# Weighed heads sent through DRAM, and a group's row shifts turned by one transpose and joined through DRAM

## The reference, cut to what matters

```
n = layernorm(x)
q, k, v = n @ Wq.T + bq, n @ Wk.T + bk, n @ Wv.T + bv        # 32 heads of 16
q, k = rope(rope(q, absolute), temporal), rope(rope(k, absolute), temporal)
w = softmax(causal(q @ k.T / 4))
x = x + layernorm((w @ v) @ Wo.T + bo)
x = x + layernorm(ffn(layernorm(x)))                          # gate, up, silu, down
```

## Time and profile before

| | |
|---|---|
| median of 3 runs | 2745.22 us |
| the profiled execution | 2745.2 us, its span 2743.5 us |
| PE / DVE / ACT / POOL busy | 92% / 77% / 52% / 36% of the span |
| attention phase | from the start to about 1700 us |
| one sequence in the middle of it | 101.09 us |
| PE and DVE busy in that sequence | 97.30 and 96.73 us |

### The profile page before, as it was taken

One profiled execution on the slowest core, in us unless ns is written; L12 is line 12 of the kernel. 1 busy time (PEld: TensorE's weight loads), 2 busy tenths in 40 slices (PEclk: granted clock), 3 DMA queues, 4 the chain that ended last, 5 costly groups with the idle time before them and its releaser, 6 DMA issues. The chain is left out here.

```text
span 2743.5 us, 55677 instructions
## 1 busy us (share of the span) xinstructions
PE 2519.6 (92%) x19584; PEld 1213.8 (44%) x19584; DVE 2122.0 (77%) x6399; ACT 1419.8 (52%) x1838; POOL 983.8 (36%) x1083
## 2 busy tenths in 40 slices
PE   3899999999999999999999996099999999999997
PEld 1444544444454454454454443044444444444443
DVE  5999999999999999999999994735555455555454
ACT  3576776776766666767676664322222222222221
POOL 4454655655565565555556553000000000000000
PEclk8999999999999999999999999599999999999999
DMA  5332433433333433433442330401121111121111
GB/s 170 98 95 76 125 92 99 122 104 94 115 105 92 117 104 92 121 102 95 123 118 77 106 96 32 191 16 46 46 76 46 46 61 46 46 76 46 46 46 46
DMA packets 125314, 236.66 MB, mean 86 GB/s; under 512 B 11441, under 2 KB 94897, under 8 KB 111921
## 3 DMA queue, kind: packets, MB, share of 16 engines
q1 hardware_dynamic: 123056, 232.84, 27.8%
q10 hardware_dynamic: 2048, 1.05, 0.1%
HBM read 148.39 MB, written 84.41 MB: 85 GB/s over the span
## 5 line engine op out<-in xcount | busy, mean ns | idle before, releaser
L655 DVE CUSTOM_DVE_ANT_0 mx<-mx,causal 128x512 f32<-128x512 f32 (+3 forms) x2048 | 944.3, 518 | 47.4 <-PE mx L785 43.4
L491 ACT ACTIVATE probs<-ts,exp_scale 128x1024 f32<-128x1024 f32 x640 | 708.8, 1107 | 325.7 <-PE ts L799 323.7
L1229 DVE SCALAR_TENSOR_TENSOR hidden<-gu,up_scale,silu 128x512 f32<-128x512 f32 x176 | 131.9, 750 | 417.7 <-PE gu L1279 407.9
L1088 ACT ACTIVATE silu<-gu,gate_scale 128x512 f32<-128x512 f32 x176 | 120.9, 687 | 631.4 <-PE gu L1279 631.4
L1063 POOL TENSOR_TENSOR f_rstd<-f_var,f_neg_half 128x4 f32<-128x4 f32 x32 | 32.3, 1009 | 928.8 <-DVE f_var L1206 647.3
L403 POOL TENSOR_SCALAR_AFFINE_SELECT probs<-probs 128x512 f32<-128x512 f32 x512 | 311.7, 635 | 145.2 <-ACT probs L491 145.2
L1277 PE MATMUL gu<-f_xT_hi,gate_hi 128*128 128x512 f16 x704 | 268.0, 381 | 51.9 <-issue 51.9
L813 PE MATMUL xb<-probs,vs 128*32 128x512 f32 (+3 forms) x4096 | 305.5, 439 | 5.0 <-ACT shift_rows L497 3.0
L382 POOL TENSOR_TENSOR turned<-biased,sin_sb 64x512 f32<-64x512 f32 x128 | 170.0, 1328 | 327.3 <-ACT biased L476 320.9
L655 DVE DVE_READ_ACCUMULATOR2_ANT row_max<- 128x1 f32 x2048 | 285.5, 139 | 0.0
L1279 PE MATMUL gu<-f_xT_lo,gate_hi 128*128 128x512 f16 x704 | 267.8, 380 | 0.0
(11 more groups left out here) (148 smaller groups left out, 4469.3 us busy)
## 6 DMA issues: line engine op xcount, KB each, us to landing
slots<-half SPq DMA_DIRECT2D x260, 128.0 KB, 12.6
qT<-slots SPq DMA_DIRECT2D x128, 256.0 KB, 3.8
kT<-slots SPq DMA_DIRECT2D x128, 256.0 KB, 4.0
xn<-x SPq DMA_DIRECT2D x16, 1024.0 KB, 9.1
xr<-x SPq DMA_DIRECT2D x16, 1024.0 KB, 6.9
slots<-half SPq DMA_DIRECT2D x256, 64.0 KB
x<-xr SPq DMA_DIRECT2D x16, 1024.0 KB, 10.8
f_xn<-x SPq DMA_DIRECT2D x16, 1024.0 KB, 4.8
```

The lines of the kernel that those rows point to most:

```text
L491: nc.scalar.activation(probs[:, g % 2, u, :, :], ts[:, :, :], ACT.Exp, scale=exp_scale[:, 0:1]).then_inc(ts_read, 1)
L655: last = nc.vector.tensor_tensor_reduce(out=scores, in0=scores, in1=causal[:, T - P * (qt + 1):T], scale=1.0, scalar=-3e38, op0=ALU.add, o ...
```

## The change

Weighed heads: the transposes to tokens by channels and back are gone. After ACT's copy to `oT`, SP writes the 128 rows to DRAM (`send_weighed`, one DMA a group). Once for two groups it reads them back with two DMAs (`fetch_weighed`): the heads' channels into `averaged`, and each head's row of sums, repeated 16 times, into `sums`. DVE takes the reciprocal of the whole `sums` tile, 128x512 (`reciprocal_of_sums`), POOL multiplies (`average`), ACT adds the bias of v and makes the high part, DVE the low part. The bias of v is so added after the weighing, and ACT, no longer DVE, copies v out of PSUM (`read_v`).

Shifts: POOL in place of DVE makes the two f16 parts, with three instructions. The columns are laid out so that one transpose gives 32 rows of 128. ACT copies them (32x128), SP writes them to DRAM (`send_shift`) and, once they have landed, reads them back as four rows of 512 into `qT` with one DMA (`place_shift`), in place of the two DMAs from ACT.

Besides: `cosine` reads the projection from PSUM and adds the bias itself; a bank of queries or keys comes free by it (`cosine_done`); `BANK_USES` has fewer entries; POOL's loop over the middle sequences is written out; the load of `xn` and the statistics of x come a step later.

```diff
+            def place_shift(i, g):
+                pairs = slice(2 * (g % 2), 2 * (g % 2) + 2)
+                sp.wait_ge(shift_out, 16 * (NG * i + g + 1))
+                sp.dma_start(qT[SHIFT_ROWS, g // 2, pairs, :],
+                             shifts[g % 2].rearrange("(p r t) k -> r p (t k)", p=2, t=NT)).then_inc(shift_in, 16)
+
+            def send_shift(i, g):
+                turned_rows, placed = held(sp, NG * i + g + 1), held(sp, 16 * (NG * i + g))
+                sp.wait_ge(shift_read, turned_rows)
+                wait_if_any(sp, shift_in, placed)
+                sp.dma_start(shifts[g % 2], shift_rows[:, g % 2, :]).then_inc(shift_out, 16)
+
+            def send_weighed(i, g):
+                ready, fetched = held(sp, NG * i + g + 1), held(sp, 32 * (NC * (i - 1) + g // 2 + 1))
+                sp.wait_ge(oT_ready, ready)
+                wait_if_any(sp, averaged_in, fetched)
+                sp.dma_start(weighed[g // 2, g % 2, :, :], oT[:, :]).then_inc(weighed_out, 16)
+
+            def fetch_weighed(i, c):
+                consumed = held(sp, NC * i + c)
+                sp.wait_ge(weighed_out, 16 * (NG * i + 2 * c + 2))
+                wait_if_any(sp, aT_ready, consumed)
+                heads = weighed[c, :, :, :].rearrange("g (h r) t -> (g h) r t", r=32)
+                sp.dma_start(sums[:, :], heads[:, DH:DH + 1, :].broadcast_to([8, DH, T])).then_inc(averaged_in, 16)
+                sp.dma_start(averaged[:, :], heads[:, 0:DH, :]).then_inc(averaged_in, 16)
...
+                    if u == 4 and exists(i + (g - 1) // NG):
+                        send_weighed(i + (g - 1) // NG, (g - 1) % NG)
                     if u == 1 and exists(i + owner):
                         send_slots(i + owner, n)
-                    if u == 2 and exists(i + owner):
+                    if u == 1 and g in FETCHED:
+                        c, of = FETCHED[g]
+                        if exists(i + of):
+                            fetch_weighed(i + of, c)
+                    if u == 2 and exists(i + (g + 1) // NG):
+                        send_shift(i + (g + 1) // NG, (g + 1) % NG)
+                    if u == 4 and exists(i + (g + 1) // NG):
+                        place_shift(i + (g + 1) // NG, (g + 1) % NG)
+                    if u == 3 and exists(i + owner):
                         fetch_slots(i + owner, n)
-                    if s == 8 and exists(i + 2):
+                    if s == 9 and exists(i + 2):
...
+            def reciprocal_of_sums(i, c):
+                dve.wait_ge(averaged_in, 32 * (NC * i + c + 1))
+                nc.vector.reciprocal(sums[:, :], sums[:, :]).then_inc(recip_done, 1)
...
-                nc.vector.tensor_tensor(roped[:, n % 2, :], biased[:, n % 2, :], cos_sb[:, :],
-                                        ALU.mult).then_inc(cosine_done, 1)
+                nc.vector.scalar_tensor_tensor(roped[:, n % 2, :], xb[:, bank_of("qk", n), :], bias_qk[:, which, ct:ct + 1],
+                                               cos_sb[:, :], ALU.add, ALU.mult).then_inc(cosine_done, 1)
...
+                nc.tensor.transpose(xb16[0:8 * NT, bank, 0:P], shift[:, :, :, :, :].rearrange("p j a l t -> p (j a l t)"),
+                                    ident16[:, :]).then_inc(shift_full, 1)
-
-            def turn_weighed(i, g):
-                bank = bank_of("o", g)
-                pe.wait_ge(oT_ready, NG * i + g + 1)
-                for t in range(NT):
-                    last = nc.tensor.transpose(xb[:, bank, P * t:P * (t + 1)], oT[:, P * t:P * (t + 1)], ident[:, :])
-                last.then_inc(o_full, 1)
```

More of the change, by code:

```diff
@@ L118, in attention_phase @@
             "p (n c o) -> p n c o", n=4, c=NC)
-        row_max = sb("row_max", [P, 2, NT, 2, 2])
-        shift = sb("shift", [P, NT, 2, 2, 2], F16)
-        shift_rows = sb("shift_rows", [P, 2, T], F16)
+        row_max = sb("row_max", [P, 2, 2, 2, NT])
+        row_shift = sb("row_shift", [P, 2, 2, NT])
+        shift = sb("shift", [P, 2, 2, 2, NT], F16)
+        shift_rows = sb("shift_rows", [8 * NT, 2, P], F16)
         oT = sb("oT", [P, T])
-        recip = sb("recip", [P, NT, HG])
-        attn = sb("attn", [P, 2, NT, P])
+        averaged = sb("averaged", [P, T])
+        sums = sb("sums", [P, T])
         y = sb("projected", [P, NT, C])
@@ L405, in mask, with shift_of_maxima, average @@
                 return masked, NT * (NG * i + g) + m + 1
+            def shift_of_maxima(i, g):
+                pool.wait_ge(mx_read, NS * i + NU * (g + 1))
+                wait_if_any(pool, shift_full, NG * i + g)
+                nc.gpsimd.tensor_scalar(shift[:, :, :, 0, :], row_max[:, g % 2, :, :, :], -1.0 / SHIFT_UNIT, None,
+                                        ALU.mult).then_inc(shift_step, 1)
+                nc.gpsimd.tensor_scalar(row_shift[:, :, :, :], row_max[:, g % 2, :, :, :], -1.0 / SHIFT_UNIT, None,
+                                        ALU.mult).then_inc(shift_step, 1)
+                pool.wait_ge(shift_step, 2 * (NG * i + g + 1))
+                nc.gpsimd.tensor_tensor(shift[:, :, :, 1, :], row_shift[:, :, :, :], shift[:, :, :, 0, :],
+                                        ALU.subtract).then_inc(shift_ready, 1)
+                return shift_ready, NG * i + g + 1
+            def average(i, c):
+                pool.wait_ge(averaged_in, 32 * (NC * i + c + 1))
+                pool.wait_ge(recip_done, NC * i + c + 1)
+                nc.gpsimd.tensor_tensor(averaged[:, :], averaged[:, :], sums[:, :], ALU.mult).then_inc(averaged_done, 1)
+                return averaged_done, NC * i + c + 1
             def residual(i, t):
@@ L417, in body @@
                     n, owner = QUERIES_KEYS[g]
+                    ahead, due = divmod(s + AHEAD - NU, NS)
+                    if u == 0 and exists(i + ahead):
+                        before = shift_of_maxima(i + ahead, due // NU)
                     if u == 0 and exists(i + (g - 1) // NG):
@@ L422, in body @@
                         before = add_turned(i + owner, n)
+                    if u == 1 and g in AVERAGED:
+                        c, of = AVERAGED[g]
+                        if exists(i + of):
+                            before = average(i + of, c)
                     if u == 4 and exists(i):
@@ L442, in _ @@
             body(1)
-            with pool.Fori(2, NB - 2) as i:
+            for i in range(2, NB - 2):
                 body(i)
@@ L839, in turn_x @@
                 last.then_inc(xT_full, 1)
-            def turn_attention(i, c, bank):
-                pe.wait_ge(o_read, NG * i + 2 * c + 2)
-                for t in range(NT):
-                    last = nc.tensor.transpose(xb[:, bank, P * t:P * (t + 1)], attn[:, c % 2, t, :], ident[:, :])
-                last.then_inc(aT_full, 1)
             def project_queries_keys(i, n, owner, part):
```

183 lines of the change are left out of this document (88 added, 95 removed).

## The result

The changed kernel takes 3013.16 us, the median of four runs (3007.61 to 3020.31), against 2745.16 us, now the median of four runs of the kernel before: a ratio of 1.0978, 95% interval 1.0954 to 1.1001. It is slower, as forecast, but by 268 us where 45 were forecast, and it lies outside the range of 2665 to 2870.

The account below looks back on a forecast made before the run. PE and DVE were taken to bound it together. Per sequence, PE 87.8 plus waits of 3.2, 10.4, 2.0 and 0.5 made 103.9 against 101.1; 2.8 x 16 = 45 us more, 2790 us, range 2665 to 2870.

Parts of the forecast that it names:

- SP's order: SP's queue: place_shift is issued only after the wait for slots, fetch_slots and send_weighed, ending at 6.4 us.
- The step by which the reciprocal makes `qk_lo` late: Odd groups' reciprocal delays qk_lo and SP in even groups; PE stalls 2.6 us at each odd group's start, 4 times a sequence.
- T: The end of a group's shift transposes, from which the forecast times the shift's trip through DRAM; 867.3 in the quiet group.
- its 7.2 us: Average time left from the end of the shift transposes until PE wants the shift in qT; odd groups stall 0 to 0.3.
- The bound of 3.8 us at most for a landing: Landing of place_shift: 2.1 us after issue, up to 3.8 if queued behind the two reads and oT's store.
- the DMA side chokes: Rival: added DMA traffic holds DVE at the reciprocal and lands shifts 1 to 2 us later; 2850 to 2873 us, chance 0.13.
- PE busy -152 us (9.5 x 16): Attention phase: removed oT, attn and shift transposes save PE 1.2 us a group, 9.5 a sequence, over 16 sequences.
- idle +197: PE waits a sequence: mx 3.2, shift 10.4, megabyte group 2.0, and 0.5 remaining of the present 3.8 idle.
- the forecast's own 0.2 a group: PE's shift transposes: four took 0.32 us to the next matmul; keeping one saves 0.2 us a group.
- 12.4 us of shift wait a sequence: PE waiting for the shift: 4 x 2.6 = 10.4 us, plus 2.0 for the group with the megabyte loads.
- Forecast -58 us over the span: DVE's busy time: gains 1.9 us a group, loses 2.36; 3.6 less a sequence, to 93.1.
- PE may be two units ahead of DVE, which absorbs most of 3.1 us: Odd groups' reciprocal: PE's lead hides most of it, leaving about 0.8 us of waiting on mx at the following u=2.

Follow-up runs that it names:

- act_sixteen: The changed kernel with the shift made the old way (four transposes, ACT's two DMAs) and reads on 16 DMA engines, reciprocal in one piece: 2915.86 us, 1.0611.
- pieces: The changed kernel with ACT's old shift, 16-engine reads, the reciprocal in four pieces of 128 columns in the even group, average and split later: 2754.86 us, 1.0031.
- filler: The changed kernel plus 14 unread matmuls (about 3 us) ahead of the wait for the shift at the start of every even group: 2977.84 us, 1.084.
- few_early: The changed kernel with ACT's old shift, reciprocals of 128x32 read back 16 times, 16-engine reads and the DMA chain begun earlier: 2725.31 us, 0.9921.

## Why the prediction was wrong

**Right.** The direction; the reciprocal (3.1 us forecast from two short rows, 3.352 measured; the estimate of 4.3 from eight cycles an element, by the repeat count that the Trainium skill gives in VectorE: DVE Perf Modes, "First, the fixed hardware budget", was further off); `cosine` at 746 ns; the stall in front of `ts` for `qT<-shifts`, four times a sequence, as the main new wait; and SP's order as what makes it late.

**Which group.** The step by which the reciprocal makes `qk_lo` late, SP's row comes at T+1.4 in every even group and PE stalls at the start of each odd one failed: the place was wrong. The stall stands at the start of the even ones. In odd groups `fetch_weighed` issues 512 KB of reads ahead of `send_shift`. I had listed those rows and let only their issue and their bytes count; the store behind them landed in 7.2 us where I had taken 2.1. "The long stall lets DVE and SP catch up, so that the odd group's own shift finds its 7.2 us enough" fell with it: the store went out at T+3 and was there at T+10 (T taken as 1005.72), where by the forecast the whole way, the read included, was to end at T+8.5.

**Landing times.** The bound of 3.8 us at most for a landing came from transfers of 256 KB that had the engines nearly to themselves. The large reads here stood behind one another with a slowest dimension of 8, and in the stall shown the second took 7.8 us and the store behind them 7.2. The rival *the DMA side chokes* named this mechanism and gave it 0.13 and 2850 to 2873; of all rivals it came nearest, and was too cheap as well.

**The size, by the page.** Forecast: PE busy -152 us (9.5 x 16), PE idle +197, sum +45. Measured: busy 0, idle +268. The larger half of the miss is in busy time.
- *The clock*, which I took as 1.00 throughout. Behind these stalls the matmuls ran at half clock. `act_sixteen` and `pieces` do the same matmuls (18816): PE is busy 2515.4 us at a clock of 0.93 and 2441.9 at 0.99 (clocks from 200 to 1600). For the changed kernel `filler` puts the loss at 62 us, and there the projection still took 402 ns (389 before, 444 in the change), so a part was left. `pieces` puts it at 78 and does three shift transposes a group more, 26 us by the forecast's own 0.2 a group: some 104, an estimate.
- *PE's saving*, forecast as 152, was then 62 to 104: the clock gave back what the work saved. I had counted the wait ahead of `oT`'s transposes as busy time, 0.18 a group or 23 us in all; where the other 25 to 67 went is not settled.
- *Idle time*: 12.4 us of shift wait a sequence make 198; measured 245.4. The rest of the 268 is small waits.

**DVE.** Forecast -58 us over the span, measured -0.6. The reciprocal's 0.25 a piece is 16 of it. The forecast added up durations, and by durations all of DVE's rows together fall by 32 us (2539.5 to 2507.0); in the records neighbouring instructions overlap, and busy time counts an overlap once, which makes up the rest. It did not decide alone, but DVE was busier than I assumed, and with a late input the reciprocal cost PE as much as the shift did. "PE may be two units ahead of DVE, which absorbs most of 3.1 us" held for the length only: with the sums in time and one piece it cost 74 us in all, 1.2 a piece (I took 0.8), but the waiting for the sums in front of it, 2.5 us in the stall shown and 94 us in all, was not in the sum.

**The steps that failed.** Two terms carry the miss of 223 us: the landing of the shift's store, priced at 2.1 us, which took 7.2 behind the large reads and put the stall in the other groups, and PE's busy time, priced at 152 us less, which stayed the same, for the larger part because the clock fell behind the stalls.

The account, in steps that the runs show: 3013 as changed; 2947 with the reads on 16 engines; 2932 with the reciprocal in pieces at a later place too (15 us, not clear of noise); 2755 with the shift on ACT again. In the other order: 3028 with the shift on ACT; 2916 with 16 engines; 2755 in pieces. No share belongs to one cause alone. What sets the price of the route (46, 92, 177) with the rest of the kernel is not settled; DVE is busier in `pieces` (2100.0 us) than in `few_early` (1933.7), but the kernel before, which pays least, is as busy (2122.0), and the bytes in SP's queue differ too; these were not separated.

## What to carry to other kernels

Before a forecast adds stalls, it should ask what each does to TensorE's clock: the stalls here, up to 5.8 us long, cost their own length and then a stretch of matmuls at half clock. A small transfer costs what stands ahead of it on its issuing engine, not what its bytes would; ask of each large one on how many engines its shape puts it. And where undoing one suspect gains nothing, undo it with the others undone: here the reciprocal's length was worth 10 us beside a late shift and 218 without.

## What the runs showed of the hardware

- A reciprocal costs by its elements: 178 ns for 4 a partition, 248 for 16, 945 for 128, 3352 for 512, some 6.3 ns for each element more (3352 - 248 over 496).
- The granted clock, 1.00 while PE worked, fell to 0.50 in a rest of 4.4 us (1013.4 to 1017.8), and stayed there until 1023, with PE at work again from 1017.8. Some 3 us of unread matmuls in front of a wait kept it at 0.99, and the kernel was 35 us faster for them.
- A store of 8 KB landed in 1.3 to 8.0 us, median 3.8; with the large reads issued behind it instead of ahead, the median was 2.1.
- The same bytes read with 16 as the slowest dimension instead of 8: 66 us off the kernel.
